# Layer norm's statistics moved from VectorE to ScalarE and GpSimd, and one subtraction from GpSimd to VectorE, in the recurrence of a six-phase network

## What is computed

```python
def _layernorm(x, axis=-1, eps=1e-05):
    m = jnp.mean(x, axis=axis, keepdims=True)
    v = jnp.var(x, axis=axis, keepdims=True)
    return (x - m) / jnp.sqrt(v + eps)

x = x + 0.5 * _L0_ffn_ref(_layernorm(x), ...)    # F: 8 gated experts, all used
x = x + _L0_attn_ref(_layernorm(x), ...)         # R: the recurrence
x = x + 0.5 * _L0_ffn_ref(_layernorm(x), ...)    # F
x = x + 0.5 * _L1_ffn_ref(_layernorm(x), ...)    # E: one expert of 8 a token
x = x + _L1_attn_ref(_layernorm(x), ...)         # M: causal attention
x = x + 0.5 * _L1_ffn_ref(_layernorm(x), ...)    # E
```

```python
def step(s, chunk):
    rr, kk, vv = chunk
    att = jnp.einsum('bhik,bhjk->bhij', rr, kk) * w_mat
    out = att @ vv + jnp.einsum('bhik,bhkv->bhiv', rr, s) * wb[None, :, :, None]
    s_new = ws[None, :, None, None] * s + jnp.einsum('bhjk,bhjv->bhkv', kk * wk[None, :, :, None], vv)
    return (s_new, out)
# y = the outs of a head / 8
mu = y.mean(-1, keepdims=True)
var = y.var(-1, keepdims=True)
y = (y - mu) / jnp.sqrt(var + EPS)     # over the 8 channels of a head
y = y * ln_w.reshape(H, K) + ln_b.reshape(H, K)
return y * g @ W_o.T                   # g = silu(xg @ W_g.T)
```

## Time and profile before

| | us |
|---|---|
| median of 3 runs | 1595.37 |
| lowest and highest of them | 1590.17, 1595.67 |
| the profiled execution | 1591.5 |
| its span, first to last instruction | 1589.6 |

### The profile page before, as it was taken

How to read it: one execution, slowest core, us unless ns; L and a number is a source line. 1 busy time by engine, 2 the same in 40 slices (tenths; PEclk the granted TensorE clock), 3 DMA queues, 4 the chain that set the end, 5 groups by cost and what they waited for, 6 DMA issues and landing times. The chain is left out here.

```text
span 1589.6 us, 43810 instructions
## 1 busy us (share of the span) xinstructions
PE 1541.5 (97%) x15808; PEld 922.1 (58%) x15808; DVE 1260.2 (79%) x2662; ACT 936.1 (59%) x1826; POOL 935.5 (59%) x806
## 2 busy tenths in 40 slices
PE   7999999999999899799999999999999999999999
PEld 4666666666666666566666666666654434444444
DVE  7976776777877788786777777768778899999877
ACT  6755555555656344365555555556553388888842
POOL 2865756757754399775766756657456334444453
PEclk9999999999999999999999999999999899999999
DMA  4300000000001242100000000000001121112011
GB/s 163 106 8 5 7 0 7 7 0 7 8 1 34 53 84 67 42 6 3 8 1 7 7 0 7 7 0 8 5 12 31 44 61 37 39 39 62 9 42 60
DMA packets 74315, 43.34 MB, mean 27 GB/s; under 512 B 53818, under 2 KB 70842, under 8 KB 74052
## 3 DMA queue, kind: packets, MB, share of 16 engines
q1 hardware_dynamic: 74180, 41.56, 10.9%
HBM read 10.47 MB, written 2.10 MB: 8 GB/s over the span
## 5 line engine op out<-in xcount | busy, mean ns | idle before, releaser
L618 POOL TENSOR_TENSOR scratch<-scratch 128x512 f16<-128x512 f32 x379 | 441.6, 1166 | 375.4 <-ACT scratch L826 375.2
L1395 DVE SCALAR_TENSOR_TENSOR scratch<-psum,scratch 128x512 f32<-128x512 f32 x512 | 352.4, 689 | 235.8 <-PE psum L1979 213.4
L821 ACT ACTIVATE scratch<-psum 128x512 f32<-128x512 f32 x512 | 305.2, 597 | 394.9 <-PE psum L1979 394.0
L2021 PE MATMUL psum<-ffn_down_hi,scratch 128*128 128x128 f16 x2048 | 369.3, 219 | 0.3
L2023 PE MATMUL psum<-ffn_down_hi,scratch 128*128 128x128 f16 x2048 | 369.2, 219 | 0.0
L2022 PE MATMUL psum<-ffn_down_lo,scratch 128*128 128x128 f16 x2048 | 369.2, 219 | 0.0
L826 ACT ACTIVATE scratch<-scratch 128x512 f16<-128x512 f32 x512 | 318.6, 622 | 12.0 <-DVE scratch L1395 11.7
L2021 PEld LDWEIGHTS psum<-ffn_down_hi,scratch 128*128 128x128 f16 x2048 | 200.3, 98 | 59.1 <-POOL scratch L618 0.7
L2022 PEld LDWEIGHTS psum<-ffn_down_lo,scratch 128*128 128x128 f16 x2048 | 200.4, 98 | 58.0
L2023 PEld LDWEIGHTS psum<-ffn_down_hi,scratch 128*128 128x128 f16 x2048 | 200.4, 98 | 0.0
L1977 PE MATMUL psum<-x_hi,ffn_gate_hi 128*128 (+1 forms) x512 | 194.5, 380 | 1.5 <-ACT scratch L821 1.5
(11 more groups left out here) (223 smaller groups left out, 2703.8 us busy)
## 6 DMA issues: line engine op xcount, KB each, us to landing
scratch<-scratch SPq DMA_DIRECT2D x96, 128.0 KB, 2.7
raw<-in_ffn_w_dram SPq DMA_DIRECT2D x8, 768.0 KB, 4.2
ffn_up_hi<-scratch SPq DMA_DIRECT2D x32, 128.0 KB, 2.8
x_tok<-in_x_dram SPq DMA_DIRECT2D x8, 256.0 KB, 7.2
out_dram<-x_tok SPq DMA_DIRECT2D x7, 256.0 KB, 2.2
raw<-in_lin_dram SPq DMA_DIRECT2D x1, 1092.0 KB
x_hi<-scratch SPq DMA_TRANSPOSE x46, 2.3
x_lo<-scratch SPq DMA_TRANSPOSE x46, 2.3
```

The source lines that it names most:

```text
L618: pool.tensor_tensor(h_lo[r], h32[r], h_hi[r], ALU.subtract).then_inc(s_plo, 1)
L821: act.activation(gate_act[k % 2], bank(k % 2), ACT.Silu, scale=W_DOWN).then_inc(s_s, 1)
L1395: dve.scalar_tensor_tensor(h32[k % HSLOTS], bank(5 + k % 2), W_DOWN, gate_act[k % 2], ALU.mult, ALU.mult).then_inc(s_h, 1)
L2021: pe.matmul(dst, h_hi[r][:, cols], hi, start=k % FC == 0 and n == 0, stop=False, skip_group_check=True)
```

## The change

In the recurrence, for the input norm of sequence b+3 (b = 0 to 6): VectorE's four bn_stats, four bn_aggr and the two small operations go. ScalarE gets `prep_sums` and `prep_squares`, eight 128x128 activations with an accumulator output, behind `gate_silu(b-1)` and ahead of `widen_rstd(b-1)`: four copies scaled by -1/128, whose sums are the negated means, then four squares with that as bias, whose sums are 128 times the variances. The second four wait for the first. GpSimd gets `prep_var`, sum of squares to variance plus epsilon, 128x4, ahead of `prep_rstd`. `x_lower` goes from the end of GpSimd's body b to VectorE's body b+1, right behind `variance(b)`. Two small tiles are new. The other phases, TensorE and SP are as before.

```diff
@@ gpsimd
+            def prep_var(n):
+                pool.wait_ge(s_mv, n + SUB)
+                pool.tensor_scalar(ln_var[:], ln_square[:], 1.0 / C, LN_EPS, ALU.mult, ALU.add).then_inc(s_var, SUB)
+
@@ gpsimd, rwkv
                     if b:
                         gn_rstd(b - 1)
                     if b + 3 < last:
+                        prep_var(n0 + SUB * (b + 3))
                         prep_rstd(n0 + SUB * (b + 3))
                         norm(b + 3)
                     if b:
                         gate_low(b - 1)
-                    if b + 3 < last:
-                        x_lower(n0 + SUB * (b + 3))
                 gn_rstd(NB - 1)
@@ scalar
+            def prep_sums(n, s):
+                act.wait_ge(s_xn, n)
+                for q in range(SUB):
+                    ins = act.activation(ln_spent[:, q * P:(q + 1) * P], sub(x_tok, s + q), ACT.Copy, scale=-1.0 / C, accum_out=ln_neg[:, q:q + 1])
+                ins.then_inc(s_bn, SUB)
+
+            def prep_squares(n, s):
+                act.wait_ge(s_bn, n + SUB)
+                act.wait_ge(s_var, n)
+                for q in range(SUB):
+                    ins = act.activation(ln_spent[:, q * P:(q + 1) * P], sub(x_tok, s + q), ACT.Square, bias=ln_neg[:, q:q + 1], accum_out=ln_square[:, q:q + 1])
+                ins.then_inc(s_mv, SUB)
@@ scalar, rwkv
                     if before:
                         gate_silu(b - 1)
+                    if b + 3 < NB + 2:
+                        if b + 3 >= NB:
+                            act.wait_ge(s_rout, b + 5 - NB)
+                        prep_sums(n0 + SUB * (b + 3), SUB * ((b + 3) % NB))
+                        prep_squares(n0 + SUB * (b + 3), SUB * ((b + 3) % NB))
+                    if before:
                         widen_rstd(b - 1)
@@ vector, rwkv
                     if before:
                         variance(b - 1)
+                        x_lower(n0 + SUB * (b + 2))
                     if more:
                         r_weighed(b + 1)
                     new_state(b, 2)
                     if before == 2:
                         add(b - 2)
                     weigh(u + 2, 2)
-                    if stats:
-                        if static and b + 3 >= NB:
-                            dve.wait_ge(s_rout, b + 5 - NB)
-                        prep_bn(n0 + SUB * b + SUB * 3, SUB * bx)
                     if more:
                         weigh_keys(u + 4, 0)
-                    if stats:
-                        dve.wait_ge(s_xn, n0 + SUB * b + SUB * 3)
                     weigh(u + 3, 3)
-                    if stats:
-                        prep_aggr(n0 + SUB * b + SUB * 3, True)
```

More of the change, by code:

```diff
@@ L111, in build @@
         ln_neg = sb("ln_neg", SUB)
+        ln_square = sb("ln_square", SUB)
+        ln_spent = sb("ln_spent", S, F16)
         minus = sb("minus", P, F16)[:]
@@ L1763, in body @@
                 def body(b, before, more):
-                    static = isinstance(b, int)
-                    stats = not static or b + 3 < (NB + 2 if ph["next"] else NB)
-                    bx = (b + 3) % NB if static else b + 3
                     u = SUB * b
```

## The result

The changed kernel takes **1596.83 us**, the median of 16 runs (1594.97 to 1600.59). The kernel before took 1594.17 (16 runs, 1590.17 to 1597.11) on the same chips. The ratio is 1.0020, with a 95% interval from 1.0012 to 1.0028: 2.7 us more, between 1.9 and 4.5. The prediction said 1598, between 1590 and 1604, with a sum of +2.7 us on the path.

What follows compares the result with a forecast made beforehand. The prediction took the chain through GpSimd's long power to bound the recurrence loop. VectorE's relief 0, the power +2.7, other GpSimd and ScalarE work 0 gave +2.7 us; set on the 1595.4 median, 1598 us, range 1590 to 1604.

Steps and rivals of the forecast that it cites:

- The bound: Recurrence loop: the chain from variance through GpSimd's 10.53 us power to normed sets the 17.31 us pass, not VectorE.
- Rival A: Recurrence loop: VectorE is the bound after all, net relief 0.8 us in seven bodies, -5.6 us, about 1590; chance 0.10.
- VectorE's relief: VectorE between variance and normed: the statistics removed, 1.47 us a body, are worth nil on the chain.
- Its sign that `normed` would wait longer: VectorE before normed: it would still wait for TensorE's transposes, and longer than the present 0.83 us.
- The price of x_lower: GpSimd's long power, held as x_lower reads SBUF on VectorE: 0.36 to 0.43 us a body, 2.7 us in all.
- Both ends of the range: Long power's delay: 0 if it reads first or has its operands, 4.7 us if it waits for x_lower whole.
- rivals B: Long power reads first and keeps the ports 10.5 us while x_lower stands: +57 us, about 1652; chance 0.03.
- D: Long power has its operands before x_lower reads, so no 2.7 us: about 1595; within the forecast's 0.77 chance.
- The rule of thumb behind the price: VectorE and GpSimd reading SBUF: the second reader waits; GpSimd is let go 0.14 us before VectorE's operation ends.
- a meeting with `gated`: GpSimd's x_norm against VectorE's two-input gated: one of four operations may differ by 0 to 0.3 us a body; taken as 0.
- The prediction's worst case: GpSimd's x_norm ends at 586.3 at worst, before ScalarE first wants it at 586.43, so covered.
- Rival C: ScalarE before the widening: accumulating activations slow, 0.9 us each, 14 us in all, about 1609; chance 0.08.

Runs made afterwards that it cites:

- statistics_only: Changed kernel with x_lower back at the end of GpSimd's body, so only the statistics move: 1594.27 us, ratio 1.0011 to the kernel before.
- x_lower_ahead: Changed kernel with x_lower right ahead of variance on VectorE instead of behind it: 1598.08 us, ratio 1.0032 to the kernel before.
- root_before: Kernel before with the seven long powers of bodies 1 to 7 replaced by ScalarE's square root and VectorE's reciprocal: 1588.03 us, ratio 0.9972.
- the half subtraction: Changed kernel with x_lower in two 256-column pieces, one behind variance, one three instructions on: 1595.18 us (one run).
- second_reader: Changed kernel with an unused 128x224 VectorE subtraction of two SBUF inputs added right behind x_lower: 1596.19 us (one run).
- x_lower_later: Changed kernel with x_lower moved three VectorE instructions on, behind r_weighed and new_state: 1593.15 us, ratio 1.0000 to the kernel before.
- x_lower_only: Kernel before with only x_lower moved to VectorE behind variance, statistics left on VectorE: 1597.79 us, ratio 1.0026.
- root_after: Changed kernel with the long powers of bodies 1 to 7 replaced by ScalarE's square root and VectorE's reciprocal: 1594.72 us, ratio 1.0007.

## Why the prediction was right, point by point

**The bound.** That the power's chain and not VectorE sets the pass was the step on which all hung, and three runs bear it out: statistics_only (1.47 us less on VectorE, nothing won), x_lower_ahead (0.6 us more on the chain, 0.6 lost) and root_before (the power gone, a pass of 16.5). Rival A is dead. The prediction called VectorE's 5.02 us from `normed` to `variance` work without a gap; in that body 0.22 us of it, before the key weighing at 567.59, is a wait for ScalarE's copy. In the next body the gap is gone, and nothing hangs on it.

**VectorE's relief.** Nil, as said. The prediction let the wait before the `weigh` grow, and it did (0.65 to 1.02, with 0.44 before the key weighing and 0.65 before the last `weigh`). Its sign that `normed` would wait longer came out by 0.04 us only, and in body 3 the other way.

**The price of x_lower.** Said: 0.36 us in the static bodies and 0.43 in those of the register loop. Measured: 0.37 to 0.38 in all seven. The extra of the register loop was an estimate from the late start of `r_weighed` (the wait computed first), and it is wrong: `x_lower` starts 0.13 us behind `variance` in a loop body (571.33 and 571.46) as elsewhere. Seven times 0.37 is 2.6 us, against 2.7. Both ends of the range that the prediction had kept, 0 and 4.7, fall with it, and so do rivals B (the powers would have come first) and D.

The rule of thumb behind the price, let go 0.14 us before the end of VectorE's operation, came from two rows of another phase. It holds in each meeting of these runs: 572.14 - 0.14 = 572.00 against 571.62 + 0.37 = 571.99 in the change, the half subtraction and second_reader within 0.01 us, and a place that the prediction missed, next.

**GpSimd.** `prep_var` takes 0.19 us, and 0.34 from its start to that of the small power, which is the delay that the prediction had put at 0.3. The four x_norm operations take 2.28, not 1.75. The prediction allowed 0 to 0.3 for a meeting with `gated` and took 0; it is 0.54 a body (the fourth reads 996 ns, where the others take 451 to 453), outside its bounds. In the trace before, the fourth ended at 585.28 and had read before `gated` began. Now it starts some 0.07 us behind `gated` (585.17, 0.74 us, two SBUF inputs) and waits until 585.17 + 0.74 - 0.14 = 585.77. What moved it is `prep_var` and not the longer power, behind which `gated` comes as well: in statistics_only, with a power of 10.53, the four take 2.28 or 2.29 us in every body. x_norm ends at 586.23, and ScalarE wants it at 586.48. The cover held with 0.25 us to spare. The prediction's worst case, 586.3, had been made for a `prep_var` of 1.01 us and no meeting, so that it held was luck.

The Trainium skill (SBUF — State Buffer, section Who interferes with whom) says that whoever issues first has the shared ports, and the other blocks. That the earlier reader holds off the other agrees with both meetings above (0.37 and 0.54 us). It says too that the first has them for its whole instruction (there of VectorE's 2-port modes, and of two SBUF inputs in the page's section SBUF: two separate sides). That doesn't hold for the power: `x_lower` ran its 0.69 us inside it in x_lower_later, and the power kept its 10.53. By second_reader the power holds VectorE for about 0.1 us.

**ScalarE.** 2.95 us against 2.8 to 3.0, and 2.70 us of the hole are left. The estimate had priced an activation at 0.3 and 0.4 and a wait between; the rows show 0.31 and 0.40, and with the accumulator's read 0.29 and 0.39 from start to start. Right in each term. Rival C is dead.

**The number.** The sum was +2.7, the passes and powers give +2.6, and the medians differ by 2.7, the last closer than their interval (1.9 to 4.5) can promise. The forecast of 1598 lay 1.2 us over the 1596.8 because it was set on the median of three runs, 1595.4, where sixteen give 1594.2.

**What stays open.** x_lower_only came out 1.3 us over what its passes say, and statistics_only's interval doesn't reach 1.0, though its passes are those of before. The runs of the kernel before alone spread from 1588.9 to 1597.6 us, and those with a mean granted clock of 0.992 average 1594.1, those of 0.995 1591.3. A straight line through 57 such runs falls by 1.0 us for each 0.001 of clock, with a scatter of 0.8 us around it. As an estimate from this line, at equal clock x_lower_later is 0.9 us over the kernel before, statistics_only 1.6, the change 3.1, x_lower_only 3.4 and x_lower_ahead 4.9, each give or take 0.3 to 1. That is 0.4 to 0.7 over what their passes and powers say (0.5, 2.6, 2.8 and 4.2), and 1.6 over for statistics_only, whose passes say nothing. So the statistics on ScalarE and GpSimd may cost something outside the passes; no run shows where, and it isn't settled. Nor is why the stretch at 1.2 GHz has another length from execution to execution.

## What to carry to other kernels

Busy shares of 89, 92 and 91% on three engines don't say which of them bounds a loop; the place where a wait closes the loop does, and work taken from another engine turns into waits there. When an operation of VectorE with two SBUF inputs is placed, look at what GpSimd starts in the 0.7 us behind it: three instructions on, the same subtraction no longer stretched the power, and what was left of its cost, 0.5 us in all, came from the load that waits for its result. So look at that too. And a hole that hides new work is a property of what makes the hole: shorten that, and the work appears on the path, as in root_after, so place it where it is free by its own neighbours.

## What the runs showed of the hardware that I had not expected

- GpSimd's power of 128x64 runs 10.53 us. A VectorE operation with two SBUF inputs that began before it holds it for what that operation has left, less 0.14 us (10.90, 10.64); one that begins 1.0 or 1.2 us into it doesn't, and isn't held itself. One that follows as the power is let go was held by about 0.1 us (0.49 us for 128x224, where 128x256 took 0.41).
- An activation with an accumulator output is two records, 0.3 to 0.4 us and a read of 0.2 us, and costs 0.29 us (copy) and 0.39 us (square with a pointer bias) from start to start at 128x128.
- A square root on ScalarE and a reciprocal on VectorE of the same 128x64 take 0.26 and 0.55 us, with two table loads on ScalarE of 1.28 us each in a body; the power takes 10.53.
- Behind the same pause of TensorE the granted clock stays at 1.2 GHz for 3.4 to 10 us, different from execution to execution of one kernel; 3.4 us more of it cost 1.7 us here.
